# LayerNorm, attention and MLP on one core: the tile turns of the first block put together, and the lower halves of V's weights moved to GpSimd

## The reference

```
xn  = (x - mean(x)) / sqrt(var(x) + 1e-5)            # per token
q, k, v = xn wq^T, xn wk^T, xn wv^T                  # 16, 4 and 4 heads of 128
q, k = rope(q), rope(k)
s   = lightning_attention(q, k, v) wo^T              # linear attention with a decay per head
g   = silu(((silu(xn W_gate * a) * (xn W_up * b)) W_down) * c)   # weights rounded to fp8 values
out = x + s * g
```

## Time and profile before

| | |
|---|---|
| median of 3 runs | 925.89 us (925.63 to 926.17) |
| the profiled execution, its time | 924.73 us |
| its span from first to last instruction | 922.9 us |
| PE busy | 97% of the span |
| DVE, ACT, POOL busy | 68%, 46%, 39% |
| PE's first instruction starts at | 9.29 us |
| V's first product starts at | 11.67 us |
| the first gate product starts at | 24.91 us |

### The profile page before, as it was taken

One profiled execution on the slowest core, in us unless ns is written; L12 is line 12 of the kernel. 1 busy time (PEld: TensorE's weight loads), 2 busy tenths in 40 slices (PEclk: granted clock), 3 DMA queues, 4 the chain that ended last, 5 costly groups with the idle time before them and its releaser, 6 DMA issues.

```text
span 922.9 us, 12461 instructions
## 1 busy us (share of the span) xinstructions
PE 899.3 (97%) x4128; PEld 738.6 (80%) x4128; DVE 627.0 (68%) x915; ACT 421.7 (46%) x709; POOL 362.2 (39%) x267
## 2 busy tenths in 40 slices
PE   5999999999999999999999999999999999999996
PEld 4888888888888878888888888878888878878776
DVE  7778653586553346666687766776866678779686
ACT  3643533443432555444455344464554454543531
POOL 1011112121122565535535545455455364554541
PEclk9999999999999999999999999999999999999999
DMA  6792213469650542331443504333423145356352
GB/s 209 226 368 91 103 46 125 174 241 326 251 205 7 199 153 110 137 121 61 145 143 119 199 23 160 135 117 136 158 81 136 38 167 205 105 181 227 115 182 81
DMA packets 51403, 138.55 MB, mean 150 GB/s; under 512 B 4256, under 2 KB 25888, under 8 KB 45984
## 3 DMA queue, kind: packets, MB, share of 16 engines
q1 hardware_dynamic: 51360, 138.00, 42.5%
HBM read 96.04 MB, written 41.94 MB: 150 GB/s over the span
## 4 chain that ended last, share of the span: by engine, by line
PE 43%; issue 30%; POOL 19%; DVE 4%; ACT 1%; DMA 1%; POOLq 0%; SPq 0%; DVEq 0%; ACTq 0%
PE bank L1210 43%; POOL d_r L1168 10%; POOL rot L1177 9%; PE bank L1257 1%; DVE d_sb L1001 1%; DMA stage<-in_x_nat 1%; DMA tail_sb<-mlp_gate 1%; DVE q_r L994 0%; DVE d_sb L1046 0%; DVE rot L987 0%; ACT d_r L682 0%; ACT gout L538 0%; DVE rot L988 0%; ACT rot L662 0%; ACT st_r L671 0%
## 5 line engine op out<-in xcount | busy, mean ns | idle before, releaser
L1210 PE MATMUL bank<-xn,aw 128*128 128x512 f32 x960 | 228.6, 389 | 0.0
L1177 POOL TENSOR_TENSOR rot<-rot 128x512 f32<-128x512 f32 x80 | 127.8, 1597 | 236.6 <-DVE rot L988 236.6
L1210 PEld LDWEIGHTS bank<-xn,aw 128*128 128x128 f32 x960 | 179.2, 188 | 36.6
L1168 POOL TENSOR_TENSOR d_r<-d_sb,d_r 128x512 fp32r<-128x512 f32 x128 | 166.6, 1329 | 51.9 <-ACT d_r L682 51.9
L1210 PE MATMUL bank<-o_r,ow 128*128 128x512 f32 (+1 forms) x816 | 186.4, 379 | 0.0
L1210 PE MATMUL bank<-xn,gu_w 128*128 128x512 f32 x768 | 179.9, 389 | 0.0
L1210 PEld LDWEIGHTS bank<-xn,gu_w 128*128 128x128 f32 x768 | 144.2, 188 | 30.1
L1210 PEld LDWEIGHTS bank<-o_r,ow 128*128 128x128 f32 x816 | 145.7, 188 | 27.5
L682 ACT CAST d_r<-d_sb 128x512 fp32r<-128x512 f32 x128 | 78.9, 621 | 100.4 <-DVE d_sb L1046 67.1
L987 DVE TENSOR_TENSOR rot<-bank,rope 128x512 f32<-128x512 f32 x80 | 55.2, 690 | 98.0 <-ACT rot L662 97.8
L661 ACT COPY rot<-bank 64x512 f32<-64x512 f32 x80 | 46.7, 584 | 145.9 <-PE bank L1210 145.4
(11 more groups left out here) (75 smaller groups left out, 946.1 us busy)
## 6 DMA issues: line engine op xcount, KB each, us to landing
xn<-xn_split SPq DMA_DIRECT2D x15, 2048.0 KB, 7.8
v_decayed<-vd_split SPq DMA_DIRECT2D x32, 512.0 KB, 3.4
vd_r<-v_decayed SPq DMA_DIRECT2D x16, 1024.0 KB, 6.9
v_r<-v_split SPq DMA_DIRECT2D x16, 512.0 KB, 5.8
wst<-in_mlp_w SPq DMA_DIRECT2D x10, 768.0 KB, 5.3
xn_split<-xn SPq DMA_DIRECT2D x3, 2048.0 KB, 10.8
stage<-in_attn_w SPq DMA_DIRECT2D x4, 1280.0 KB, 6.1
stage<-in_x_nat SPq DMA_DIRECT2D x16, 256.0 KB, 4.7
```

What stands on the lines that cost most here:

```text
L1168: pool.tensor_tensor(d_r[:, slot(e), 1, :], d_sb[:, slot(e), :], d_r[:, slot(e), 0, :].bitcast(F32), ALU.subtract).then_inc(d_lo, 1)
L1177: pool.tensor_tensor(rot1[:, r % RRING, :], rot1[:, r % RRING, :], rot2[:, r % RRING, :], ALU.add).then_inc(qk_sum, 1)
L1210: last = pe.matmul(dst, a, b, start=start and x == 0, stop=stop and x == len(pairs) - 1)
```

## The change

Three edits, all in the ramp:

1. TensorE turns all four tiles of the first block, and only then starts V's products: all four upper products, then the four rests as before.
2. The four `wv_split_lo` leave VectorE's queue and go to GpSimd's, between its second and third `power`.
3. On VectorE, `w_round(1)` moves from behind the second block's `inv_std` to directly behind `w_round(0)`, ahead of two `tile_stats`.

```diff
@@ VectorE
-            def wv_split_lo(k):
-                dve.wait_ge(wv_hi, k + 1)
-                dve.tensor_tensor(wv[:, 1, k, :], wv_raw[:, k, :], wv[:, 0, k, :].bitcast(F32), ALU.subtract).then_inc(wv_lo, 1)
...
             norm(3)
-            wv_split_lo(0)
-            wv_split_lo(1)
-            norm_lo(0)
-            wv_split_lo(2)
-            wv_split_lo(3)
-            for i in range(1, TT):
+            for i in range(TT):
                 norm_lo(i)
             w_exponent(0)
             w_exponent(1)
             tile_stats(TT)
             tile_stats(TT + 1)
             w_round(0)
+            w_round(1)
             tile_stats(TT + 2)
             tile_stats(TT + 3)
             mean_var(2)
             v_rest(0)
             inv_std(2)
-            w_round(1)
@@ GpSimd
+            def wv_split_lo(k):
+                pool.wait_ge(wv_hi, k + 1)
+                pool.tensor_tensor(wv[:, 1, k, :], wv_raw[:, k, :], wv[:, 0, k, :].bitcast(F32), ALU.subtract).then_inc(wv_lo, 1)
+
             power(0)
             power(1)
+            for k in range(KT):
+                wv_split_lo(k)
             power(2)
@@ TensorE
-            ln_transpose(0)
-            ln_transpose(1)
-            v_first_high(0)
-            ln_transpose(2)
-            v_first_high(1)
-            ln_transpose(3)
-            v_first_high(2)
-            v_first_high(3)
+            for i in range(TT):
+                ln_transpose(i)
+            for v in range(TT):
+                v_first_high(v)
```

## The result

| | before | changed |
|---|---|---|
| median | 925.89 us (924.65 to 926.34, 5 runs) | 929.85 us (928.57 to 930.78, 5 runs) |
| the profiled execution | 924.73 us, span 922.9 us | 928.57 us, span 926.8 us |
| ratio to before | | 1.0044, 95% interval 1.0029 to 1.0059 |

The kernel is 0.44% slower, clear of the 0.2% that a measurement here can tell. 930.9 us had been forecast, in a range of 929.0 to 932.4. The loss of 4.0 between the medians and of 3.8 between the profiled executions is the same one.

The account below looks back on a forecast made before the run. TensorE (PE), busy 97% of the span, was taken as the bound. Held inv_std, later turns and slow-clock matmuls moved the first gate product from 24.91 to 29.95, +5.0 on the 925.89 median: 930.9 us, range 929.0 to 932.4.

Parts of the forecast that it names:

- The hold: Second inv_std on VectorE: each of its four tiny instructions waits for a whole GpSimd subtraction, ending at 14.9 instead of 10.48.
- The sum: Ramp up to the first gate product: its start moves from 24.91 to 29.95 us, +5.0 us, giving 930.9 us.
- Subtractions: GpSimd from 9.7 us: four times 1.29 plus about 0.02 each, so L784 ends at 14.9 and norm 2 starts at 14.95.
- The turns: TensorE's turns of tiles 2 and 3 run 15.6 to 17.35; without the hold, turning early gains 0.2 to 0.3 us.
- The clock: TensorE's rise to 2.4 GHz comes 5.1 us after its restart at 15.6, at 20.7; 7.8 of V's 48 matmuls run slowly.
- its lower bound: Clock rising before V's first matmul in the ramp: 1.6 us less, +3.4 instead of +5.0.
- The edits that were to be worth nothing: In the ramp: fewer VectorE instructions and the moved w_round(1) bring nothing, early turns hardly anything, 0.2 to 0.3 us.
- The sentence that it would matter only by its own 1.4 us: VectorE: without cover, w_round(1)'s two instructions would stand between V and the up side, some 1.4 us.
- The variant in which a norm is not held: L776 slips in ahead of subtraction 0, norm 2 unheld ends at 14.2: +3.7, 929.6 us, chance 0.10.
- The tiny instructions: Rival: the chain slips through before GpSimd's hold; with only L776 held +0.4 to +1.0, 926.6 us; chance 0.06.
- With two held, about +2.2: Same rival with two of the inv_std chain's instructions held: 928.1 us; a third of its 0.06 lies beyond 1.9 us.
- the two don't meet: Rival: the subtractions start behind the inv_std chain, after 10.5 us; gain of 0.2 to 0.3 us, 925.6 us; chance 0.10.

Follow-up runs that it names:

- Run 1: Kernel before with only the four subtractions moved to GpSimd; TensorE's order and w_round(1) as before: 928.34 us, ratio 1.0031.
- run 3: Changed kernel with GpSimd's first subtraction waiting until the inv_std chain of tiles 2 and 3 has ended: 927.44 us, ratio 1.0024.
- run 4: Changed kernel with subtractions 0 and 1 directly behind power, 2 and 3 waiting for the end of the inv_std chain: 929.76 us, ratio 1.0048.
- Run 2: Kernel before with only TensorE's new order, four turns and then V's upper products; subtractions stay on VectorE: 925.51 us, ratio 1.0000.
- run 9: Changed kernel with the subtractions waiting until norm 3 has ended and w_round(1) back behind the second block's inv_std: 925.51 us, ratio 0.9998.
- run 10: Kernel before with only w_round(1) moved directly behind w_round(0): 926.90 us, ratio 1.0013.
- run 5: Changed kernel with GpSimd's first subtraction waiting until norm 3 has ended: 926.42 us, ratio 1.0007.
- run 6: Changed kernel with 20 unused transposes of the identity matrix on TensorE between turns 1 and 2: 927.74 us, ratio 1.0023.

## Why the prediction was right

**The hold.** "L776 waits for subtraction 0, L778 for 1, L781 for 2, L784 for 3" happened to the piece, and GpSimd was first, at 9.68 against 9.73. Run 1 has the same hold by GpSimd's edit alone, run 3 takes it off the whole chain, and run 4 off two of the four. It could be read from before's trace alone: one held L776 at 94.39 us was the whole mechanism, in another block. What makes the one engine wait for the other is not seen in the trace; it shows only who is late and by how much.

**The sum**, +5.0 us forecast, +3.89 in the profile and 3.96 between medians. By terms:
- Subtractions: forecast 1.31 apart, measured 4.93 us for four, 1.23 apart. L784 ends at 14.63 instead of 14.9, norm 2 starts 0.29 earlier than forecast.
- The turns: forecast 15.6 to 17.35, measured 15.26 to 16.88. Together with the term above, 0.47 us.
- The clock, the largest miss: I let it rise 5.1 us behind TensorE's restart. It rose about 3.5 us behind it (18.8 against 15.26), so that some 4.5 instead of 7.8 matmuls ran slowly and the 48 took 11.92 instead of 12.60 us: 0.68 us. The rise lay between the forecast's middle and its lower bound (before V's first matmul). To carry 5.1 us over from one rise was a guess: in the profiles of runs 2 and 9, which do the same work up to V, it came some 5.5 and 4.4 us behind the first turn.
- 0.47 + 0.68 = 1.15 is the difference between +5.0 and +3.9. Both misses went the same way and used up more than half of the 1.9 us between the forecast and the lower end of its range.

**The edits that were to be worth nothing.** The turns: 0.2 to 0.3 us to be won without the hold. Run 2's 0.19 agrees by luck: run 9, with the same TensorE queue, stands 0.5 us better for the clock's rise alone, and the times tell neither from before. `w_round(1)`: free in the changed kernel, as said. The sentence that it would matter only by its own 1.4 us between V and the up side named the wrong victim: run 10 shows that it holds up the second block's `inv_std` and all that hangs on it, at a like price.

**The norms.** The variant in which a norm is not held (929.6) was given 0.10, with the remark that the trace spoke weakly for it. Run 3 shows that they are held. It made no difference to the changed kernel, where the subtractions were over at 14.6 when norm 2 started, and all the difference to the first repair.

**The rivals.** The tiny instructions did not slip through. The price of that rival was too low all the same: it let the norms pass ("With two held, about +2.2"), and run 4, with two of the chain held, lost 3.2 us, since the other two subtractions held the norms. That the two don't meet is what run 5 had to make by a wait; it gives back all but 0.5 us in the profile, which lies in the wait that the third edit makes, and with run 9 the time is that of before (0.9989 to 1.0007).

## What to carry to other kernels

- Before a GpSimd instruction is put beside a chain of small VectorE instructions, look in the trace for one VectorE instruction that overlaps a GpSimd one and took much longer than its like. While GpSimd's queue is full, the price is one GpSimd instruction for each VectorE instruction that is held, however small it is: here a chain of four took 4.9 us instead of 0.74. Held were those with two SBUF inputs, norms and exponent masks; `norm_lo` and the statistics were not (see below).
- Moving work to an idle engine needs a time for it as well as an engine: behind the chain's end and the norms it was harmless (run 9), 1.9 us earlier it cost 4 us. An order that puts a consumer in front of work that could fill its wait leaves the engine idle in it: 0.9 us of such work here, and up to 1.7 more by the clock.
- A pause of TensorE early in a kernel can cost clock besides the work that it displaces: 1.7 us of 3.9 behind a pause of 4.0 here, and none in run 1's profile behind one of 1.8. A repair should be followed to the next wait behind it: two repairs here (runs 3 and 5) uncovered another.

## What the runs showed of the hardware

- GpSimd and VectorE alternate by whole instructions. Four subtractions held four VectorE instructions in the changed kernel and in runs 1 and 4, and two in run 3, where two of them met only `norm_lo`. A tiny instruction ends within 0.02 us of the subtraction's end and costs GpSimd nothing: the four subtractions take 1258 to 1268 ns beside it, less than the 1290 of the earlier trace rows. Held norms cost GpSimd something too: the first three subtractions of run 3 took 4.09 us, against 3.7 for three in the changed kernel.
- The hold also takes norms (3.00 us for two instead of 1.00) and the exponent masks L811 (1.30 and 1.52 us instead of 0.42), which both read a single SBUF tensor. `norm_lo`, with one input in PSUM, ran beside the subtractions at 675 to 691 ns in run 3. Nor is every instruction that reads one SBUF tensor held: in the kernel before, two `tile_stats` ran within one GpSimd subtraction in their usual time, 1.28 us for two (VectorE, then GpSimd):

```profile
76.26 1.28 DVE L760 BATCH_NORM_STATS2 stats<-stage 128x6 f32<-128x512 f32 x2
76.21 1.29 POOL L1149 TENSOR_TENSOR fsplit<-fz,fsplit 128x512 fp32r<-128x512 f32 x1 [7.77 <-ACT fsplit L531]
```
- TensorE's rise to 2.4 GHz came 5.1 us after its first work in the kernel before, and 3.5 us after the restart at 15.26 in the changed one, behind 4 us of pause. What it did in the pause mattered: with filler (run 6) it ran the turns at 15.43 at 2.4 GHz, 1.11 us for eight. In run 1 it ran them so behind a pause of 1.79 us as well, 0.66 us for four.
- The first tile lands at a different time in each execution: the first turn came between 9.29 and 9.93 us in these thirteen profiles.
